# Sixteen scattering transfers on one queue, with a wait between groups of four

## What is computed

```python
dist2 = jnp.sum((x[:, :, None, :] - keys) ** 2, axis=-1)
logits = -dist2 + jnp.einsum('bld,ed->ble', x, rw) + rb
topv, topi = jax.lax.top_k(logits, 4)
w = jax.nn.softmax(topv, axis=-1)
hidden = gelu(jnp.einsum('bld,efd->blef', x, w1) + b1)   # f = 1024
exp_out = jnp.einsum('blef,edf->bled', hidden, w2) + b2
fused = sum of w * exp_out over the 4 chosen experts
```

## Time and profile before

| | us |
|---|---|
| runs before, median of 3 | 764.39 |
| lowest, highest | 757.75, 767.33 |
| profiled execution, span from first to last instruction | 778.8 |
| GpSimd's 16 scatters, first to last start | 291.49 to 310.98 |

### The profile page before, as it was taken

The page is one execution under the profiler, slowest core; times in us unless marked ns, Lnnn a source line. Parts: engine busy times, 40 slices in busy tenths (PEclk is TensorE's granted clock), DMA queues, the critical chain, the costliest instruction groups (busy, mean ns, idle before and its releaser), DMA issues.

```text
span 778.8 us, 15559 instructions
## 1 busy us (share of the span) xinstructions
PE 705.9 (91%) x5728; PEld 572.2 (73%) x5728; DVE 537.9 (69%) x1189; ACT 414.7 (53%) x786; POOL 431.0 (55%) x451
## 2 busy tenths in 40 slices
PE   5799999999998866999999999996989779889987
PEld 2577777778776766899999999973464446657677
DVE  4688778778787474047777777716555978887576
ACT  3565665665654331366666666531338956664332
POOL 4648644645644117467778888544022859984130
PEclk9999999999999877899999999998999999999999
DMA  8201101101020396879989999987523500001000
GB/s 333 98 2 56 56 1 54 54 0 54 0 109 2 130 406 274 314 260 409 371 331 341 344 333 336 365 332 273 218 77 112 227 0 1 1 0 42 1 0 28
DMA packets 20476, 123.50 MB, mean 159 GB/s; under 512 B 2288, under 2 KB 6784, under 8 KB 13120
## 3 DMA queue, kind: packets, MB, share of 16 engines
q1 hardware_dynamic: 17488, 114.72, 38.8%
q0 software_dynamic: 2928, 8.00, 2.8%
HBM read 111.90 MB, written 10.81 MB: 158 GB/s over the span
## 4 chain that ended last, share of the span: by engine, by line
PE 73%; DVE 10%; ACT 6%; issue 4%; POOL 3%; another core or an unknown queue 1%; DMA 1%; SPq 0%; DVEq 0%; ACTq 0%; PEldq 0%
PE banks L2049 63%; PE banks L2118 7%; POOL inject L985 1%; DMA ctx_raw<-in_ctxT 1%; ACT probs L1049 1%; DVE negmax_raw L1503 1%; DVE banks L1930 1%; PE banks L2563 1%; DVE shown L1919 1%; ACT banks L1291 1%; PE banks L2286 1%; ACT ctx_hi L1035 1%; DVE X L2008 1%; DVE shown L1940 0%
## 5 line engine op out<-in xcount | busy, mean ns | idle before, releaser
L2049 PE MATMUL banks<-xT,raw 128*128 128x128 f32 x992 | 152.3, 277 | 0.6 <-DVE xT L1718 0.6
L2049 PEld LDWEIGHTS banks<-xT,raw 128*128 128x128 f32 x992 | 135.7, 193 | 3.3 <-issue 1.2
L918 POOL TENSOR_TENSOR w_lo<-raw,w_hi 128x1024 fp32r<-128x1024 f32 x50 | 118.0, 2387 | 1.7 <-ACT w_hi L1142 1.0
L1173 ACT ACTIVATE banks<-banks,later 128x128 f32<-128x128 f32 x200 | 67.9, 340 | 56.2 <-PE banks L2049 55.0
L985 POOL TENSOR_TENSOR inject<-BCbc,drive 128x1024 f32<-128x1024 f32 x32 | 74.9, 2358 | 20.2 <-DVE drive L1877 9.5
L1078 ACT ACTIVATE probsT<-banks 128x512 f32<-128x512 f32 x64 | 38.3, 598 | 85.2 <-PE banks L2118 85.0
L1724 DVE CAST mid_hi<-banks 128x128 fp32r<-128x128 f32 x200 | 57.8, 289 | 33.6 <-ACT banks L1173 31.9
L1503 DVE TENSOR_REDUCE negmax_raw<-banks 128x1 f32<-128x1024 f32 x64 | 77.5, 1211 | 2.8 <-PE banks L2049 2.8
L1049 ACT ACTIVATE probs<-banks,negmax 128x1024 f32<-128x1024 f32 x64 | 71.2, 1113 | 10.9 <-DVE negmax L1505 10.7
L2118 PE MATMUL banks<-table,probs 128*128 128x128 f32 x512 | 71.0, 283 | 2.1 <-DVE probsT L1476 2.1
L2049 PE MATMUL banks<-w_hi,mid_hi 128*128 128x256 f32 x200 | 72.6, 363 | 0.0
(11 more groups left out here) (344 smaller groups left out, 1787.9 us busy)
## 6 DMA issues: line engine op xcount, KB each, us to landing
raw<-in_w SPq DMA_DIRECT2D x31, 2048.0 KB, 8.4
ctx_raw<-in_ctxT SPq DMA_DIRECT2D x8, 1024.0 KB, 4.8
ctxT<-in_ctxT SPq DMA_DIRECT2D x4, 2048.0 KB, 10.5
ctxN<-in_ctxN SPq DMA_DIRECT2D x4, 2048.0 KB, 11.0
x_slots<-zero SPq DMA_DIRECT2D x1, 3968.0 KB, 12.1
y_slots<-y_tile POOLq DMA_DIRECT2D x29, 128.0 KB, 7.1
wf<-in_w SPq DMA_DIRECT2D x9, 384.0 KB, 5.3
BCbc<-bc_rows SPq DMA_DIRECT2D x6, 512.0 KB, 7.3
```

What stands on the lines that cost most here:

```text
L918: nc.gpsimd.tensor_tensor(w2_lo[i % WB][:, cols], raw[i % WB][:, EW // 2:][:, cols], w2_hi[i % 2][:, cols].bitcast(F32), ALU.subtract).the ...
L1173: nc.scalar.activation(to, held, ACT.Gelu, bias=b1[:, bass.ds(at + u, 1)]).then_inc(gelu_done, 1)
L2049: return nc.tensor.matmul(o, lhsT, rhs, start=start, stop=stop)
```

## The change

GpSimd waits ahead of the second, third and fourth group of four scatters until all earlier ones have landed (`scattered` at 64, 128, 192).

```diff
--- before.py
+++ after.py
@@ -906,6 +906,8 @@
             pool.wait_ge(zeroed, 32)
             pool.wait_ge(slots_ready, 1)
             for t in range(TC):
+                if t:
+                    pool.wait_ge(scattered, 16 * TOP0 * t)
                 for j in range(TOP0):
                     k = TOP0 * t + j
                     nc.gpsimd.indirect_dma_start(x_slots, bass.IndirectOffsetOnAxis(slots[:, k:k + 1], 0), xn[:, t, :], None)\
```

## The result

The changed kernel takes 772.56 us (median of 4 runs, 769.96 to 775.51), the kernel before 765.31 beside it: ratio 1.0125, interval 1.009 to 1.016. So it is slower by a little over 1%, 7 us by the medians. I had forecast 764.4, a cost of nothing; the 8.2 us to the measured time have to be found.

The account below looks back on a forecast made before the run. The prediction took TensorE, busy 91% of 778.8 us, as the bound. Scatters landing 7.1 us later were to cost 0 in GpSimd's queue and 0 in SyncE's, leaving 764.4 us, range 755.5 to 773.

Parts of the forecast that it names:

- GpSimd's waits really bite; the gaps: GpSimd's queue between scatter groups: the first gap about 5 us, the others about 1.3 us.
- A group takes 6.05 us, last landing 2.1 us after its last issue: Each later scatter group: 0.15 us release, 3.8 us of steps, 2.1 us to landing; three groups 18.2 us.
- x_rows wanted at 327.9: TensorE's first turn of x_rows in the timeline without the stall: 335.42 less 7.5 us.
- x_rows lands 3 us after its load: SyncE's first x_rows load, with no load ahead of it: 3 us taken, between 1.6 and 9.6, landing at 323.3.
- a cover of 4.6: Slack in us between x_rows landing at 323.3 and TensorE wanting it at 327.9, so the later load costs 0.
- x_rows late: Rival at SyncE's x_rows load: waited groups land in 7.1 us, tile 4 waits, 765 to 784 us; chance 0.07.
- stretched stall: Rival at TensorE under the scatters: the stall is in the runs and lasts 7.1 us longer, 769.9 us; chance 0.18.
- The stall belongs to the profiled execution: TensorE's idle time under scatters and gathers was held mostly absent from the timed runs, so it costs them hardly anything.
- 15.7 and 14.4 us: TensorE's idle time under scatters and gathers (7.5 + 8.2), against the profiled execution's excess over the runs' median.
- Relief: Rival at TensorE under the scatters: scatters in flight cause the stall, emptying the queue avoids it, 756.9 us; chance 0.11.
- item (a): GpSimd's own queue behind the scatters: stores, masks and the weights' low half, wanted from 328.2, stay on time; cost 0.

Follow-up runs that it names:

- e_two: The kernel before with one wait in the middle of the scatters, making two groups of eight: 766.8 us, ratio 0.9896 to the kernel before.
- e_hot5: The changed kernel with a fifth tile picked by TensorE from xn (HOT = 5): 771.7 us, ratio 1.007 to the kernel before.
- e_two_behind: The kernel before with two groups of eight scatters and expert 5's load moved behind the x_rows loads: 766.6 us, ratio 1.0018.
- c0_before: The kernel before, unchanged, profiled once more: 774.3 us, ratio 1.002.
- c0_fourth: The kernel before, unchanged, run and profiled again in sitting 5: 774.0 us, ratio 0.998.
- e_load_behind: The changed kernel with expert 5's load moved behind the two x_rows loads: 767.8 us, ratio 0.994 to the kernel before.

## Why the prediction was wrong

- *GpSimd's waits really bite; the gaps.* Right for the first (5.42 us for about 5) and the third (1.72 for 1.3), wrong for the second (5.42 for 1.3).
- *A group takes 6.05 us, last landing 2.1 us after its last issue.* This is the first step that failed. I took 2.1 us for all later groups since "only one [load] comes back". That one, expert 5's, came back exactly beside group 2: 6.4 us. I had it 7 us later (307.3) because I shifted the timeline by too little. x_rows' load went 33.4 us after the first scatter, not 28.8: 4.6 us, of which the second gap alone is 4.1.
- *x_rows wanted at 327.9.* The second step that failed, and the largest term. I took only the 7.5 us of visible idle time off the first profile's 335.42. Left in were 5.1 us of work at half clock: 2.0 ahead of the stall and 3.1 in and behind it. Wanted: 31.3 us after the first scatter, not 36.4.
- *x_rows lands 3 us after its load.* 3.8: 0.8 us.
- Together 4.6 + 5.1 + 0.8 = 10.5 us against a cover of 4.6: 5.9 us of idle time, which is what TensorE waited, and 1.6 at half clock. The mechanism was the rival *x_rows late*, which I had at 0.07, with its decision point at a group of 7.6 us: too far off, for the same reason, since I computed the cover in the wrong timeline. That 772.56 still lies in my range, 755.5 to 773, is luck: its upper end was put there for the stretched stall and the spread of the runs, and neither is what happened.
- *The stall belongs to the profiled execution.* Wrong, and shown wrong. All five profiles of the kernel before have it, four of them in executions that are among those timed. The near equality of 15.7 and 14.4 us was chance: I compared one execution (781.0 us as the runs are timed) with three runs that it was not among, and never asked what else could part them. The Trainium skill's rule on back pressure ("NOTIFIC — the notification-queue block", Interfaces) gave this no support: the stall goes with a break in the row of scatters, in executions with the same profiling. Whether that block has a part in it, no run shows.
- *Stretched stall* is refuted: spreading the scatters did not stretch the stall, it removed it. *Relief* was half right: it came on occasions where the kernel before lies near 773, and there pays for the late x_rows (ratio 0.9964). Its reason, scatters in flight, is not borne out: I had the stall set in around 300, but TensorE's idle time begins at 303.2, and by 304 the packets of eight to nine of the ten scatters issued had moved (413 packets at 48 each); e_two has the same backlog (190 packets moved 9.5 us after its first scatter, where this kernel had 193) and idles 0.37 us. It is not excluded either.
- The cost of GpSimd's queue, item (a), "On time, with no air left", was right: e_hot5 shows it as the next bound.

What stays open: why the kernel before lies at 764 to 765 us in sittings 1 and 3 and 773 to 780 in five others. That it has little of the stall there fits: without it, it would lie beside e_two_behind, and it does, within 0.2%. But no profile of it from such a sitting exists; this is argued, not shown, and with it why the change cost 1% in those sittings and nothing in sitting 5. Another cause of short executions does stand in the profiles. The profiled one of c0_before was the shortest of its ten runs, 768.08 us, and has the stall all the same, a stage of 41.4 us. Its time is made up later: its gathers go out in 22.2 us and 231.4 follow behind the last, where c0_fourth takes 26.5 and 235.4. A stretch of 20 us, 120 us behind the last gather, in c0_before and in c0_fourth:

```profile
654.50:674.50 20.00, 17.35 (x101) 12.80 (x100) 18.57 (x11) 12.89 (x21) 19.86 (x12) 1.00 0.00 1
...
657.20:677.20 20.00, 17.52 (x88) 12.51 (x89) 16.89 (x11) 12.43 (x21) 19.17 (x12) 0.91 0.00 1
```

The granted clock is 1.00 in the one and 0.91 in the other, and 101 matmuls are done against 88. Over all profiles the time behind the last gather lies between 231 and 238 us, with or without the stall. So single spans do not follow the stage, and a part of the difference between sittings may lie there; no experiment has parted the two. What in the chip holds TensorE and ScalarE back under a long row of indirect transfers is open too.

A version better than the changed kernel is at hand, two groups of eight: 766 to 767 us in two sittings, under every median of the changed kernel, though never beside it. Against the kernel before it gains 1% where that one lies near 773; where it lies near 764, the nearest run, e_two_behind, ties.

## What to carry to other kernels

Before a wait is priced at nothing, work out the cover in the timeline of an undisturbed stage: take out a stall's idle time and also the half clock behind it, and let the loads move up with it, since one of them may land beside the very transfers that are now waited for. A latency is read from a row with the same neighbours. If a long row of indirect transfers from GpSimd stands in the kernel, try a break in its middle, by a wait or by a piece of GpSimd's own work (766.0 and 768.2 us in the same sitting here), and time the kernel before in several sittings before a per cent is believed.

## What was not expected of the hardware

- Under an unbroken row of 16 scatters TensorE and ScalarE stood still in all five profiles, from the ninth or tenth scatter on (idle pieces of 0.2 to 3.9 us), until about the last one; the stage was 9.5 to 13.6 us longer than 31.3, 7.5 to 11.0 of it by the stall. With rows of four it never came, with rows of eight the pieces were 0.2 to 1.8 us, with twelve 2.05 and 2.41. Ahead of one product under the 16 gathers, which no experiment touched, TensorE stood still 2.8 to 8.2 us in 14 of the 19 profiles and 0.5 us in the other five; what decides between them is not known. GpSimd went on at 1.27 us a scatter through it, and the DMA engines were at 0.31 of their share.
- A group of four scatters (512 KB) landed 2.7 us after its last issue in quiet and 6.4 us with one 2 MB load beside it; with that load moved away (e_load_behind) the same group took 3.3.
